# Attention, LoRA projection and expert routing on one core: the second batch's logits from one product per token tile, with the last attention outputs in a row

## What is computed

```python
# batch b picks one expert by argmax(cond_8[b])
y = (silu(x @ wu.T + bu) * (x @ wg.T + bg)) @ wd.T + bd                 # gated MLP
Q, K, V = heads(y @ Wq.T + bq), heads(y @ Wk.T + bk), heads(y @ Wv.T + bv)   # 16 heads of 8
scores = conv1d_over_keys(Q @ K.T / sqrt(8), conv_w, taps=3) + conv_b   # mixes the heads
o = softmax(scores) @ V
x = x + (o @ Wo.T + bo)                                                 # x1
z = x @ W_base.T + b_base + 2 * sum_e w[b,e] * (x @ As[e].T) @ Bs[e].T  # LoRA mixture
gates = softmax(z @ wg)                      # 8 experts, 1024 tokens
expert_idx = argmax(gates)
pos = cumsum(one_hot(expert_idx)) - 1        # place in the expert's queue, over both batches
keep = pos < 128                             # capacity: 128 tokens for each expert
disp[expert_idx, pos] = z * keep
eo = relu(disp @ w1 + b1) @ w2 + b2
x = x + eo[expert_idx, pos] * max(gates) * keep
```

## Time and profile before

| what | value |
|---|---|
| median of three executions | 242.76 us |
| the profiled execution's own time | 242.87 us |
| span of its trace | 241.0 us |
| PE, DVE, ACT, POOL busy | 224.5, 195.2, 165.0, 161.5 us |
| first attention scores (L1040) start | 22.49 us |
| last attention product (L920) ends in the chain | 204.25 us |
| first expert layer (L1119) starts in the chain | 218.57 us |
| eight output DMAs (L338) start | 223.52 to 237.10 us |

### The profile page before, as it was taken

One profiled execution on the slowest core, in us unless ns is written; L12 is line 12 of the kernel. 1 busy time (PEld: TensorE's weight loads), 2 busy tenths in 40 slices (PEclk: granted clock), 3 DMA queues, 4 the chain that ended last, 5 costly groups with the idle time before them and its releaser, 6 DMA issues.

```text
span 241.0 us, 5432 instructions
## 1 busy us (share of the span) xinstructions
PE 224.5 (93%) x1733; PEld 177.3 (74%) x1733; DVE 195.2 (81%) x486; ACT 165.0 (68%) x297; POOL 161.5 (67%) x189
## 2 busy tenths in 40 slices
PE   8997987899989989999999999999999989999980
PEld 7444765687868868888876886788788876688980
DVE  2469999979889998997998999989979782385570
ACT  2645669989698779988978479799798670313510
POOL 1029768999878969998886478899983600051785
PEclk9999999999999999999999999999999999999996
DMA  6990003764636536563545353546556530930233
GB/s 201 347 411 0 0 1 133 175 184 169 132 131 131 194 67 201 190 134 132 129 155 110 136 128 132 133 174 158 143 181 133 185 78 4 334 101 3 22 33 33
DMA packets 14933, 32.77 MB, mean 136 GB/s; under 512 B 1586, under 2 KB 11826, under 8 KB 14642
## 3 DMA queue, kind: packets, MB, share of 16 engines
q1 hardware_dynamic: 13330, 31.35, 43.4%
q0 software_dynamic: 1152, 0.52, 2.5%
q10 hardware_dynamic: 432, 0.65, 0.8%
HBM read 19.67 MB, written 13.37 MB: 137 GB/s over the span
## 4 chain that ended last, share of the span: by engine, by line
PE 67%; DVE 11%; issue 8%; POOL 4%; ACT 4%; DMA 2%; SPq 1%; POOLq 1%; DVEq 0%; ACTq 0%
PE tp L1019 12%; PE sc L879 11%; PE sc L881 10%; PE sc L880 9%; PE pvbank L900 6%; PE pvbank L898 5%; POOL out L338 4%; DVE Pb L600 3%; PE sc L1073 2%; DMA we<-in_wexp 2%; PE sc L1074 1%; ACT Kh L393 1%; PE misc L926 1%; ACT PT L442 1%; DVE kc L536 1%
## 5 line engine op out<-in xcount | busy, mean ns | idle before, releaser
L398 ACT ACTIVATE Pb<-Pb,nbias 128x512 f32<-128x512 f32 x128 | 90.5, 718 | 26.7 <-DVE Pb L600 25.6
L600 DVE TENSOR_SCALAR_CACHE_REDUCE Pb<-sc,col 128x512 f32<-128x512 f32 x128 | 91.6, 733 | 10.4 <-PE sc L881 10.2
L879 PE MATMUL sc<-Kh,Ql 128*128 128x512 f32 x124 | 57.0, 460 | 2.5 <-POOL Kl L262 1.4
L1019 PE MATMUL tp<-cst,Pb 128*128 128x128 f32 x332 | 49.9, 273 | 3.9 <-ACT PT L442 3.1
L1019 PEld LDWEIGHTS tp<-cst,Pb 128*128 128x128 f32 x332 | 40.5, 140 | 16.8 <-issue 4.2
L881 PE MATMUL sc<-Kh,Qh 128*128 128x512 f32 x124 | 48.9, 394 | 0.0
L880 PE MATMUL sc<-Kl,Qh 128*128 128x512 f32 x124 | 48.8, 393 | 0.0
L262 POOL TENSOR_TENSOR Kl<-kc,Kh 128x512 fp32r<-128x512 f32 x28 | 36.1, 1288 | 18.6 <-ACT Kh L393 17.4
L442 ACT ACTIVATE PT<-tp 128x512 f32<-128x512 f32 x79 | 45.9, 581 | 1.6 <-PE tp L1019 1.0
L274 POOL TENSOR_TENSOR td<-ta,tc_ 128x512 f32<-128x512 f32 x31 | 44.0, 1418 | 2.6
L267 POOL TENSOR_SCALAR ta<-Kp,cwS 128x512 f32<-128x512 f32 x31 | 23.4, 754 | 13.8 <-ACT Kp L371 13.6
(11 more groups left out here) (214 smaller groups left out, 287.5 us busy)
## 6 DMA issues: line engine op xcount, KB each, us to landing
swap<-w2s SPq DMA_DIRECT2D x15, 768.0 KB, 3.3
PT<-swap SPq DMA_DIRECT2D x60, 192.0 KB, 3.8
w1s<-in_w SPq DMA_DIRECT2D x1, 2048.0 KB, 10.0
w2s<-in_w SPq DMA_DIRECT2D x1, 2048.0 KB, 8.0
cst<-in_consts SPq DMA_DIRECT2D x1, 652.0 KB, 5.6
xTs<-in_xT SPq DMA_DIRECT2D x2, 256.0 KB, 3.1
we<-in_wexp SPq DMA_DIRECT2D x2, 256.0 KB, 3.4
b2s<-in_b2row SPq DMA_DIRECT2D x1, 512.0 KB, 10.7
```

Of the source, the lines that this page charges most:

```text
L398: act.activation(Pb[:, k, :], Pb[:, k, :], ACT.Exp, bias=nbias[:, k:k + 1], scale=-1.0)\
L600: dve.tensor_scalar(Pb[:, k, :], SC[k % 4][:, :], cb, None, ALU.subtract, ALU.min, accum_out=nbias[:, k:k + 1]).then_inc(s["mx"], 1)
L879: pe.matmul(SC[k][:, :], ql, Kh[:, h2, :], start=True, stop=False)
L1019: mm = pe.transpose(bank[:, k * 128:(k + 1) * 128], Pb[:, u % RING, k * 128:(k + 1) * 128], ident)
```

## The change

Seven things change together; the diff below is cut to them.

1. **Logits from one product per token tile.** For batch 1, `weff` and `wz` get eight more columns ahead of their 128: the same weight applied to the gate matrix. With x (now with bo added, `xb`) and the attention output as weights, four products each of 128x136 give the logits and z at once, with tokens on the partitions (`project_x`, `project_o`), in a two-bank tile `LZ`. The steps 2, 3 and 5 of batch 1 are gone from PE. The base bias enters the logits by a small product (`gate_base`) and z only at the copies to `DT`.
2. **Output projection.** Step 1 is four products with the attention output as weight, which gives tokens directly; x comes in token order from memory (a transfer of 512 KB), bo is added by POOL, and step 4 is gone.
3. **Last outputs in a row.** The turns of units 12 to 15 go into the score banks, `outputs` of the last group is split in two around the turn of unit 15, both `last_outputs` follow each other, and what stood between them moves behind. On DVE the D tiles and Zl of batch 0 move behind the last unit.
4. **Expert choice on logits.** The mask comes from the logits' maximum; the exponential, its sum and the gate value come later (step 13). The gate value is the reciprocal of the sum.
5. **Counts.** The counts of batch 0 are put into batch 1's accumulation ahead of the mask.
6. **Experts.** `first_up` stands after one dispatch of half 1 instead of two and writes two banks, the first copy of `DT` has 128 columns, the copy of half 1 moves to ACT, `b2` is weighted before the product arrives, so that one instruction instead of two follows `down`.
7. **Front.** `wz` is made in the front, with two further small products and copies for the eight columns; ACT adds bo to x at units 4 and 6.

```diff
-AT_PE = {(0, 5): 12, (0, 10): 0, (0, 12): 2, (0, 14): 3, (1, 1): 6, (NG - 1, 13): 5}
-AT_ACT = {(0, 11): 0, (0, 13): 2, (0, 15): 3, (NG - 1, 14): 5}
-AT_DVE = {(0, 6): 12, (0, 15): 3, (1, 2): 6, (1, 9): 8, (NG - 1, 10): 9, (NG - 1, 12): 10,
-  (NG - 1, 14): 5}
+AT_PE = {(0, 10): 0, (0, 12): 2, (0, 14): 3, (1, 1): 6, (NG - 1, 13): 5}
+AT_ACT = {(0, 11): 0, (0, 13): 2, (1, 0): 3, (NG - 1, 14): 5}
+AT_DVE = {(0, 15): 3, (1, 2): 6, (1, 4): 13, (1, 9): 8}
...
+def turn_bank(b, g, u):
+    if last_pair(b, g, u):
+        return SC[u % 4] if u >= 12 else TP[u % 2]
+    return TP[by_pe(0, 0, u) % 2]
...
+    sp.dma_start(X1[:, :, :], xtok.rearrange("(t p) c -> p t c", p=128)).then_inc(s["xtk"], 16)
+    sp.wait_ge(s["wte"], 1)
+    sp.dma_start(bor, borow).then_inc(s["xtk"], 16)
...
+    pool.wait_ge(s["ones"], 1)
+    pool.wait_ge(s["wte"], 1)
+    pool.tensor_scalar(bbr, ones[:, :], col[:, BB:BB + 1], 1.0, ALU.mult, ALU.mult).then_inc(s["bbb"], 1)
...
+        if b:
+            pool.wait_ge(s["xtk"], 32)
+            bo = lo_w[:, 2:3, :].broadcast_to([128, NT, C])
+            pool.tensor_tensor(X1[:, :, :], X1[:, :, :], bo, ALU.add).then_inc(s["xto"], 1)
...
+    act.wait_ge(s["lam"], 1)
+    act.activation(weff[:, :, 0:E], SC[3][:, 0:B * E].rearrange("p (b e) -> p b e", b=B), ACT.Copy)\
+        .then_inc(s["lae"], 1)
...
+    act.wait_ge(s["wzm"], 1)
+    act.activation(wz[:, :, :].rearrange("p b m -> p (b m)"), PV[:, 0:B * W], ACT.Copy).then_inc(s["wze"], 1)
...
+        elif u in (4, 6):
+            at = slice(S * (u // 2 - 2), S * (u // 2 - 1))
+            act.wait_ge(s["mlp"], 4 * B)
+            act.activation(xb[:, at], xb[:, at], ACT.Identity, bias=col[:, BO:BO + 1]).then_inc(s["xbo"], 1)
...
-    after(1, 0)
-    after(0, 4)
-    for k in (2, 3, 4, 5):
+    for k in (0, 5, 3):
         after(1, k)
 
+    base = col[:, BB:BB + 1]
     act.wait_ge(s["dsp"], 1)
-    act.activation(DT[:, 0:512], SC[0][:, :], ACT.Copy).then_inc(s["dtea"], 1)
+    act.activation(DT[:, 0:CAP], SC[0][:, 0:CAP], ACT.Identity, bias=base).then_inc(s["dtea"], 1)
+    act.activation(DT[:, CAP:512], SC[0][:, CAP:512], ACT.Identity, bias=base).then_inc(s["dtea"], 1)
...
+    hidden(2)
+    act.wait_ge(s["dsp"], 2)
+    act.activation(DT[:, 512:1024], SC[1][:, :], ACT.Identity, bias=base).then_inc(s["dted"], 1)
...
-            dve.wait_ge(s["wo"], b + 1)
-            dve.scalar_tensor_tensor(x1T, bank[:, :], col[:, BO:BO + 1], xTs[:, S * b:S * (b + 1)],
-                                     ALU.add, ALU.add).then_inc(s["x1"], 1)
+        if k == 1:
+            dve.wait_ge(s["wo"], B - b)
+            dve.wait_ge(s["xto"], 1)
+            dve.tensor_tensor(X1[:, tiles, :], bank[:, :].rearrange("p (t m) -> p t m", t=QT), X1[:, tiles, :],
+                              ALU.add).then_inc(s["x1"], 1)
...
+                dve.tensor_copy(L, LZ[:, :, 0:E]).then_inc(s["lgc"], 1)
+                dve.wait_ge(s["lgc"], 1)
             step(dve.tensor_reduce(lmax, L, AX.X, ALU.max))
-            dve.tensor_tensor(lg[:, :, :], L, over_experts(lmax), ALU.subtract).then_inc(s["nl"], 1)
-            dve.wait_ge(s["nla"], b + 1)
-            dve.tensor_reduce(gmax, es[:, :, :], AX.X, ALU.max).then_inc(s["gm"], 1)
-            step(dve.tensor_reduce(ssum, es[:, :, :], AX.X, ALU.add))
-            step(dve.reciprocal(rs, ssum))
-            dve.tensor_tensor(es[:, :, :], es[:, :, :], over_experts(rs), ALU.mult).then_inc(s["gm"], 1)
-            dve.wait_ge(s["gm"], 3 * b + 1)
-            dve.tensor_tensor(gval[:, tiles], gmax, rs, ALU.mult).then_inc(s["gm"], 1)
-            dve.wait_ge(s["gm"], 3 * b + 3)
-            step(dve.tensor_tensor(eq[:, :, :], es[:, :, :], over_experts(gval[:, tiles]), ALU.is_equal))
+            step(dve.tensor_tensor(eq[:, :, :], L, over_experts(lmax), ALU.is_equal))
 
...
+        elif k == 13:
+
+            dve.wait_ge(s["nla"], b + 1)
+            step(dve.tensor_reduce(ssum, es[:, :, :], AX.X, ALU.add))
+            dve.reciprocal(gval[:, tiles], ssum).then_inc(s["gm"], 1)
         elif k == 6:
             dve.wait_ge(s["cum"], b + 1)
...
+    after(0, 9)
+    after(0, 5)
+    after(0, 10)
+    after(0, 11)
     dve.wait_ge(s["pv"], 4 * NG + 1)
     dve.wait_ge(s["otr"], B * NG)
     dve.tensor_copy(RAW[:, 0:384], PV[:, 0:384]).then_inc(s["raw"], 1)
+    dve.wait_ge(s["pv"], 4 * NG + 2)
+    dve.tensor_copy(RAW[:, 384:512], TP[0][:, 0:128]).then_inc(s["raw"], 1)
+    normalise(1, NG)
+    for k in (3, 5, 6, 1):
+        after(1, k)
     after(0, 1)
-    dve.wait_ge(s["pv"], 4 * NG + 2)
-    dve.tensor_copy(RAW[:, 384:512], SC[3][:, 0:128]).then_inc(s["raw"], 1)
-    normalise(1, NG)
-    after(0, 11)
-    for k in (1, 3, 5, 6):
-        after(1, k)
     dve.wait_ge(s["slt"], 2)
     for h in range(2):
         for t in range(QT, NT):
+            if (h, t) == (1, QT):
+                after(1, 13)
             dve.tensor_scalar(D[:, t, 512 * h:512 * (h + 1)], cst[:, IOTA + 512 * h:IOTA + 512 * (h + 1)],
                               slot[:, t:t + 1], None, ALU.is_equal).then_inc(s["disp1"], 1)
-    dve.wait_ge(s["dsp"], 2)
-    dve.tensor_copy(DT[:, 512:1024], SC[1][:, :]).then_inc(s["dted"], 1)
+    dve.wait_ge(s["hmm"], 1)
+    for j in range(NJ // 2, NJ):
+        dve.tensor_scalar(HT[0][:, j, :], PV[:, (j - 2) * 128:(j - 1) * 128],
+                          col[:, B1 + j:B1 + j + 1], 0.0, ALU.add, ALU.max).then_inc(s["hevx"], 1)
...
+    def weighted_bias(e):
+        dve.tensor_scalar(EO[:, e, :], b2s[:, e * C:(e + 1) * C], held[:, e:e + 1], None, ALU.mult)\
+            .then_inc(s["b2g"], 1)
...
-        dve.tensor_tensor(EO[:, e, :], TP[e % 2][:, 0:C], b2s[:, e * C:(e + 1) * C], ALU.add)\
-            .then_inc(s["eo"], 1)
-        weighted(e)
+        dve.wait_ge(s["b2g"], e + 1)
+        dve.scalar_tensor_tensor(EOg[:, e, :], TP[e % 2][:, 0:C], held[:, e:e + 1], EO[:, e, :],
+                                 ALU.mult, ALU.add).then_inc(s["eog"], 1)
+        if e + 1 < E:
+            weighted_bias(e + 1)
...
+    pe.wait_ge(s["wefe"], B)
+    for b in range(B):
+        mm = pe.matmul(MISC[:, (B + b) * C:(B + b + 1) * C], bs[:, b, :], lo_w[:, 0, :], start=True, stop=True)
+    mm.then_inc(s["wtm"], 1)
...
+    for b in range(B):
+        mm = pe.matmul(SC[3][:, b * E:(b + 1) * E], weffT[:, b, :], col[:, WG:WG + E], start=True, stop=True)
+    mm.then_inc(s["lam"], 1)
...
+    pe.matmul(PV[:, 0:B * W], wq[:, 4, :], weff[:, :, :].rearrange("p b m -> p (b m)"), start=True, stop=True)\
+        .then_inc(s["wzm"], 1)
...
-        bank = (PV[:, 256:384], SC[3][:, 0:128])[l]
+        bank = (PV[:, 256:384], TP[0][:, 0:128])[l]
...
+    def project_x(q):
+
+        pe.matmul(LZ[:, q, 0:W], xb[:, S + 128 * q:S + 128 * (q + 1)], weff[:, 1, :], start=(q % 2 == 0), stop=False)
+
+    def gate_base():
+
+        for i in range(2):
+            pe.matmul(LZ[:, 2 * i:2 * i + 2, 0:E], bbr[:, :],
+                      col[:, WG:WG + E].rearrange("p (a e) -> p a e", a=1).broadcast_to([128, 2, E]),
+                      start=False, stop=False)
+
+    def project_o():
+
+        pe.wait_ge(s["ote"], B)
+        for q in range(QT):
+            mm = pe.matmul(LZ[:, q, 0:W], OT[:, 128 * q:128 * (q + 1)], wz[:, 1, :], start=False, stop=(q % 2 == 1))
+        mm.then_inc(s["lgm"], 1)
 
-            pe.wait_ge(s["ote"], b + 1)
-            pe.matmul(bank[:, :], wq[:, 3, :], turned[b], start=True, stop=True).then_inc(s["wo"], 1)
+            for q in range(QT):
+                mm = pe.matmul(bank[:, q * 128:(q + 1) * 128], turned[b][:, q * 128:(q + 1) * 128], wq[:, 3, :],
+                               start=True, stop=True)
+            mm.then_inc(s["wo"], 1)
...
-            mm = pe.matmul(at, tri_r[:, :], mask[:, QT * b:QT * (b + 1), :], start=True, stop=False)
-            for p in range(QT * (b + 1) - 1):
-                first = max(p + 1 - QT * b, 0)
+            mm = pe.matmul(at, tri_r[:, :], mask[:, QT * b:QT * (b + 1), :], start=(b == 0), stop=False)
+            for p in range(QT * b, QT * (b + 1) - 1):
+                first = p + 1 - QT * b
                 mm = pe.matmul(at[:, first:, :], ones_r[:, :],
                                mask[:, p:p + 1, :].broadcast_to([128, QT - first, E]),
                                start=False, stop=(p == QT * (b + 1) - 2))
...
+    def first_batch_counts():
+
+        at = STAGE_BANK[1][6][:, 64:64 + QT * E].rearrange("p (t e) -> p t e", e=E)
+        for p in range(QT):
+            pe.matmul(at, ones_r[:, :], mask[:, p:p + 1, :].broadcast_to([128, QT, E]),
+                      start=(p == 0), stop=False)
...
-    for u in range(NG * U):
+    for u in range(NG * U - 1):
         unit(1, u // U, u % U)
+    outputs(2 * (B * NG - 1), 0, B * NG - 1, (0, 1))
+    unit(1, NG - 1, U - 1)
+    outputs(2 * (B * NG - 1), 0, B * NG - 1, (2, 3))
     pe.wait_ge(s["mx"], U * NG * B + 1)
-    after(0, 1)
     last_outputs(0)
+    last_outputs(1)
...
-    pe.wait_ge(s["zlo"], 1)
```

(51 more changed lines are left out.)

225 lines of the change are left out of this document (120 added, 105 removed).

## The result

The changed kernel takes 238.63 us (median of 4 runs, 238.41 to 238.91) against 242.72 us (241.66 to 242.88) for the kernel before in the same session: a ratio of 0.984, with a 95% interval from 0.981 to 0.987. That is 4.1 us or 1.6% faster, more than the 0.5% that can be told from no change. The prediction was 237.9 us. The profiled execution took 238.91 us, with a span of 236.7 us.

A forecast was written before the change was run, and what follows sets the result against it. PE's product list, then the output DMAs' own pace, was taken to bound the tail. From the profiled 242.87 us, 4.95 less in the tail and 0.0 elsewhere gave 237.9 us; own range 236.6 to 239.2, 8 in 10 235.8 to 240.3.

The forecast's parts named there:

- Part 1: Last attention products: moved PE work and waits for copies of turned units go; 3.5 us gained, ending at 200.75.
- Part 2: From the last attention products to the turned O: nothing gained or lost, ACT's copy ends at 203.55.
- Part 6: Front, middle and additions of bo: gains and costs together 0.0 us.
- Part 3: From the turned O to the mask: six DVE steps at 0.22 us, mask at 206.25, 3.1 us gained.
- Part 4: From mask to first expert layer: PE's list is the bound, 1.5 us given back, `first_up` at 213.5.
- Part 5: From first expert layer to output DMAs: first at 218.1, last begins at 232.15 instead of 237.10.
- the rule on the shared port: Beside POOL's sum of bo: DVE instructions with two SBUF inputs would wait up to 2.6 us; PSUM reads escape it.
- less is gained: Rival, chance 0.14: last turns keep their waits (+1.2) and ACT's additions cost their full 1.2 (+0.7); 239.8 us.
- slower: Rival, chance 0.05: in the tail from 206 us, TensorE's clock falls from 2.4 to 1.2 GHz; 248 us with 10 us.
- more is gained: Rival, chance 0.10: seams cost less and DVE's relief in the middle counts, 236.2 us; w2's transfer limits further gain.

The follow-up runs named there:

- e5: Changed kernel with the turns of units 12 to 15 alternating between the two shared TP banks again; 240.50 us, ratio 0.991 to the kernel before.
- e6: Changed kernel with two D tiles and Zl of batch 0 back between the last head's copies on DVE; 239.36 us, ratio 0.984 to the kernel before.
- e7: Changed kernel with batch 1's subtraction, exponential, sum and reciprocal ahead of the mask again; 240.16 us, ratio 0.989 to the kernel before.
- e8: Changed kernel with batch 1's z computed in channels again; 241.14 us, ratio 0.994 to the kernel before.
- e2: Changed kernel with four unread 128x512 additions on DVE between slot and batch 1's D tiles; 239.97 us, ratio 0.988 to the kernel before.
- e4: Changed kernel with ACT's two additions of bo moved to the idle time behind the first keys; 238.40 us, ratio 0.981 to the kernel before.
- e1: Changed kernel with the three filler products put back ahead of the last dispatches; 239.85 us, ratio 0.987 to the kernel before.

## Why the prediction was right, point by point

The mechanism of the tail held: the end follows PE's list and the DMAs behind it. Part 1 names one cause too many, part 2 left a pair of products out, and part 6 fits only as a sum. Predicted 232.15 us for the start of the last DMA, measured 232.89; the 0.74 us are made up as follows. The profiled execution took 238.91 us where 237.9 was predicted, so 0.25 us more lie behind that start. They come from outside the trace: the device time is 2.2 us longer than the span after the change and 1.87 before, which the prediction left equal and whose cause stays open.

- **Part 1, right in size, half wrong in its reason.** Predicted end of the attention products 200.75, measured 201.06. Of the 0.31 us, 0.27 come from before 189.8 us, so the part itself gave 3.46 of 3.5. The waits of the turns went, but by the banks (e5: 1.4 to 1.6 us); DVE's relief, which the prediction named beside them, gave nothing with the banks in place (e6).
- **Part 2, the term that was mis-sized.** RAW's turn, x and base products, O's turn and its copy: predicted 2.80 us, measured 201.06 to 204.19, 3.13. The prediction let RAW's turn take the same 0.75 us as before, which held a wait for the copy of RAW. In that wait now stand the first two x products, and they are longer than it: 0.66 for the pair and 0.44 for the turn, 1.10 in place of 0.75. The second pair took the 0.48 that was counted (0.47), the base products 0.35 where I had counted 0.48, and O's turn 0.58 instead of 0.47. So the pair that the sum left out makes up the error: 0.17 us at its cadence (0.48 + 0.44 - 0.75) and 0.18 as the seam behind the attention products.
- **Part 3, right.** From OT to the mask 2.60 us, predicted 2.70: six DVE steps 0.22 us apart. e7 and e8 show that what is added to this path is paid.
- **Part 4, right.** From the mask to `first_up` 7.19 us, predicted 7.25. The mask was 6.05 us earlier and `first_up` 4.6: PE's list took back 1.5, as predicted, with one gap of 0.15 us ahead of the mask's products. The first D tile had 1.2 us to spare (e2), predicted 1.1; the sums of X stand ahead of it and cost nothing.
- **Part 5, right, 0.26 long in sum.** `first_up` to the first DMA 4.80 (predicted 4.6), first to third 4.71 (4.8), third to last 9.40 (9.25). The 0.2 us of the first are `first_up`, which took 0.70 + 0.45 us over its two banks and not 0.92. The third waited for `down(2)`, as said.
- **Part 6, right only as a sum.** Predicted 0.0, measured +0.27 at 189.8 us. The terms as written (0.8 and 0.2 less, 0.3 and 0.5 more) make -0.2; they make 0.0 only if the 0.24 of the base product is counted beside the 0.2. Step 12 gave its time (from the copy near 102 to that near 123 us: 20.25 against 21.17 before, 0.92 less; predicted 0.8), ACT's additions cost 0.5 as predicted (e4). The front was put at 0.3; from the first-layer products to the first scores it took 12.76 us against 12.82 before, so nothing, and the first scores came 0.37 us later because those products began 0.43 us later. Step 3 was to give 0.2, and the stretch that holds it, from the copy near 123 to that near 149 us, is 0.16 longer (25.50 against 25.34). Four stretches that hold no term of the sum differ by -0.27 to +0.57 us, most of all the last (20.89 against 20.32), within what it varies by. That all this comes to 0.27 is luck.
- **POOL's sum of bo** took 2.40 us, from 190.90, where 2.6 was estimated. DVE's copies beside it read PSUM and kept their length (0.69 us at 191.43, as at 194.31 in the earlier trace rows), so that no run here tests the rule on the shared port that the prediction names.

Of the rivals, *less is gained* needed the turns' waits (none left) and the full 1.2 us of the additions (0.5); *slower*, by the clock, is out by e1 and the clock of 1.00 up to 230 us. w2 was fetched from 201.10 us and took 7.6 us, to 208.7, and PE needed it only behind 211.5, so that *more is gained* was not stopped there; but the seams cost more and not less than I had counted.

## What to carry to other kernels

Where one engine works through a full list, price each edit by that engine's time between the events that bound the list, and count the seams: in these traces a group behind attention products with 32 columns of weights, in front of such products, behind products of 8 to 24 columns, or behind a wait took 0.1 to 0.25 us more than its cadence. Not every change of kind pays: the dispatch behind O's turn took its 0.23 us a product, the products with O behind it 0.97 for 0.96. And count each product that moves into a wait against the wait's length. A wait that the profile puts down to the last semaphore can be caused by the bank that the instruction writes; here a bank of its own for each of the last four turns took away 1.4 to 1.6 us of waiting, and a copying engine with less to do took away none beside that. And two stretches between events of each trace told effects of 0.3 us apart that the medians of five or six runs, spread over up to 3 us, did not; it takes such a stretch to repeat (T within 0.03 us), and the one ahead of 189.8 us does not.

## What the runs showed of the hardware that was not expected

- Two base products of 16 columns took 0.35 us (L1011), 0.17 each, where four products of 136 columns took 0.97 (L1019), 0.24 each: a short product costs far more than its share of columns. The four weight loads of the base products, 128 columns each, took 0.53 us beside them, as those of two x products did.
- The last five output DMAs keep a pace of 1.88 us for 128x128 words on average, and PE needs 2 x 0.89 us for the two layers of an expert (L1226), so that the two are nearly tied. By my estimate from these two, 1.88 - 1.78, a PE list shortened only behind the third DMA would bring little; no run tried it.
- POOL's four `hot` tiles took 3.41 us beside DVE's D tiles, 2.70 beside sums and then D tiles in the kernel after, and 2.36 in e2, where all of DVE's work beside them but the small steps were sums that read a bank.
